# Four probability-value steps of a head pair in one block, and the output projection one round earlier

## The chip, the cores and the metric

One core of a Trainium2 chip runs the kernel. The time is device microseconds (us) of one execution; lower is better. The engines are TensorE (PE, its weight loads are shown as PEld), VectorE (DVE), ScalarE (ACT), GpSimd (POOL) and SyncE (SP), which issues most DMAs. Each runs its own list of instructions in the order written; semaphores order them against each other.

## The reference

A transformer block with adaptive layer norm on x of 4 batches x 512 tokens x 128 features, float32. Cut to what matters here:

```python
h = layernorm(x) * (1 + ca) + sa
qkv = h @ qkv_w.T                              # 16 heads of 64
scores = q @ k.T * 64 ** -0.5 + bias           # bias: 32 relative-position buckets per head
a = softmax(scores) @ v
x = x + ga * (a @ o_w.T)
h = layernorm(x) * (1 + cb) + sb
x = x + gb * experts(h)                        # 160 experts of 64, 8 per token, and a shared one
```

## The kernel before

The kernel has two phases. Attention comes first, for some 480 us; then routing, and a loop over pairs of experts. The change is in attention only.

**Tiling.** Attention works on pairs of heads: 8 pairs in each of 4 batches, 32 in a row. A pair has 8 units: 2 heads x 4 query tiles of 128 rows. For one unit:

- PE (`scores`, L407, matmuls L415 and L417) writes 128 x 512 scores to one of two PSUM banks; it waits until the bias of the unit two before is done.
- DVE (`add_bias`, L1018, instruction L1032) adds the position bias, writes `prob` in SBUF and keeps the row's extreme.
- ACT (`exponential`, L727, instruction L729) takes the exponential in place and, with a second small instruction, reads the row's sum.
- DVE (`invert_sums`, L1043, instruction L1049) inverts the sums of two units at once.
- POOL (`normalise`, L900, instruction L904) scales the unit.
- PE (`transpose_probs`, L420, instruction L426) transposes it in 4 parts into one of two PSUM banks.
- ACT (even units) or DVE (odd units) copies that bank to `PT` (`copy_probs`, L732 and L1037, both recorded at L208).

When all 8 units of a pair are in `PT`, PE runs four probability-value steps (`attend`, L430, matmuls L439), one for each tile of 128 keys. Each has two heads, whose matmuls write different halves of one bank; all four add into the same bank. DVE copies the result to `oT` (`copy_o`, L1051), and PE multiplies it with the pair's part of the output weights (`project_out`, L447, matmul L452), which adds the 8 pairs of a batch in one bank.

**Order.** Nothing is scheduled by a planner. Each engine has a function `pair(b, n)` that writes its order by hand, in four rounds of two units each; each round starts with the scores, biases and exponentials of its two units. Work of the pair before fills in: the transposes and copies of its units 4 and 5 are in round one, of 6 and 7 in round two; units 0 and 1 of the pair itself are transposed in round three, 2 and 3 in round four. Further in the rounds:

- `project_v` (PE, round two, L400), copied by ACT (`copy_v`, L738) ahead of ACT's copy of unit 6.
- `project_qk` for the pair after next (PE, round four, L389); then ACT's `qk_high` (L720, instruction L725) and DVE's `qk_low` (L1013, instruction L1015), and SP's DMAs that stack q and k. ACT runs `qk_high` after exponential 7; DVE runs `qk_low` as the last of the pair, and the next pair's bias of unit 0 behind it.
- Value steps: steps 0 and 1 of pair n-1 in round three of pair n; steps 2 and 3 in round one of pair n+1. The first step waits for the copies of units 6 and 7 and for `copy_o` of the pair before.
- `copy_o` in round one on DVE, `project_out` in round two on PE.
- At a batch's end the output is gated (`gate_y`, DVE), transposed back (`transpose_y`, PE) and added to x (`update_x`, DVE); in the next pair DVE takes the new x's statistics (`new_statistics`).

Pairs 8 and 9 of a batch in the code (`n` = 8 and 9) are pairs 0 and 1 of the next batch. The last batch has a short form (`final`), and the tail after it is written out.

Of the kernel before, what the change touches and what calls it, by code (L numbers as in the profile page):

```python
# [25 lines left out]
B, S, D = 4, 512, 128  # L26
# [6 lines left out]
QT = S // P  # L33
NT = T // P
HPAIRS = H // 2
# [20 lines left out]
def adaln_block(nc, x, emb, qkv_t, o_t, router_t, expert_bias, gate_t_in, down_t, gate_shared_t,  # L56
# [12 lines left out]
    with ctx:  # L69
# [284 lines left out]
        def _(pe):  # L354
# [75 lines left out]
            def attend(b, n, kb):  # L430

                if kb == 0:
                    for unit in (UNITS - 2, UNITS - 1):
                        pe.wait_ge(*copied(b, UNITS * n + unit))
                    pe.wait_ge(s_vc, b * HPAIRS + (2 * (n // 2) + 2))
                    if n >= 1:
                        pe.wait_ge(s_o, b * HPAIRS + n)
                for head in range(2):
                    last = nc.tensor.matmul(  # L439
                        ps[head * HD:(head + 1) * HD, BANK_O, :],  # L440
                        v_sb[:, (n // 2) % 2, kb, (n % 2) * P + head * HD:(n % 2) * P + (head + 1) * HD],
                        PT[:, n % 2, (head * QT + kb) * S:(head * QT + kb + 1) * S],
                        start=kb == 0, stop=kb == QT - 1, skip_group_check=True)
                if kb == QT - 1:
                    last.then_inc(s_pv, 1)

            def project_out(b, n):  # L447
                hp = n % HPAIRS
                pe.wait_ge(s_o, b * HPAIRS + (n + 1))
                if hp == 0:  # L450
                    pe.wait_ge(s_x2, b + (n // HPAIRS + X2_AHEAD))
                nc.tensor.matmul(ps[:, BANK_Y, :], woT[:, hp, :], oT[:, n % 2, :], start=hp == 0,  # L452
                                 stop=hp == HPAIRS - 1, skip_group_check=True).then_inc(s_ymm, 1)

            def transpose_y(b):

                pe.wait_ge(s_yg, b + 1)
                for t in range(QT):
                    last = nc.tensor.transpose(ps[:, BANK_Y, t * P:(t + 1) * P], yT[:, t * P:(t + 1) * P], ident[:, :])
                last.then_inc(s_ytr, 1)  # L460
# [58 lines left out]
            def pair(b, n, final=False):  # L519

                scores(b, n, 0)
                scores(b, n, 1)
                if n >= 2:
                    attend(b, n - 2, 2)
                    attend(b, n - 2, 3)
                if n == 0:
                    project_qk(b, 1)
                if n >= 1:
                    transpose_probs(b, n - 1, 4)
                    transpose_probs(b, n - 1, 5)  # L530

                scores(b, n, 2)
                scores(b, n, 3)
                if n == 0:
                    pe.wait_ge(w_split, 3)
                    project_v(b, 0)
                if not (final and n >= HPAIRS - 1):
                    project_v(b, n + 1)
                if n >= 2:
                    project_out(b, n - 2)  # L540
                if n >= 1:
                    transpose_probs(b, n - 1, 6)
                    transpose_probs(b, n - 1, 7)

                scores(b, n, 4)
                scores(b, n, 5)
                if n >= 1:
                    attend(b, n - 1, 0)
                    attend(b, n - 1, 1)
                transpose_probs(b, n, 0)  # L550
                transpose_probs(b, n, 1)

                scores(b, n, 6)
                scores(b, n, 7)
                if n == HPAIRS + 1:
                    transpose_y(b)
                if not (final and n >= HPAIRS - 2):
                    project_qk(b, n + 2)
                if final and n == HPAIRS - 1:
                    transpose_normed(0)  # L560
                transpose_probs(b, n, 2)
                transpose_probs(b, n, 3)
# [14 lines left out]
                    pair(b, n)  # L577
            for n in range(2, HPAIRS):
                pair(B - 1, n, True)
            attend(B - 1, HPAIRS - 2, 2)  # L580
            attend(B - 1, HPAIRS - 2, 3)
            transpose_probs(B - 1, HPAIRS - 1, 4)
            transpose_probs(B - 1, HPAIRS - 1, 5)
            project_out(B - 1, HPAIRS - 2)
# [339 lines left out]
        def _(dve):  # L924
# [30 lines left out]
            def qkv_low(n):  # L955

                k = QKV_STEPS[n]
                dve.wait_ge(w_high, n + 1)
                nc.vector.scalar_tensor_tensor(
                    out=wT[:, LOW, k * 512:(k + 1) * 512], in0=qkv_in[:, k * 512:(k + 1) * 512],  # L960
                    scalar=HD ** -0.5 if k < 2 else 1.0, in1=wT[:, HIGH, k * 512:(k + 1) * 512].bitcast(F32),
                    op0=ALU.mult, op1=ALU.subtract).then_inc(w_split, 1)
# [13 lines left out]
            def first_low(n):  # L976
                b = FIRST_ORDER[n]
                modulated_low(n, hcur if b == 0 else hT[:, b, :, :], h_full[b])
# [58 lines left out]
            def copy_probs(b, n, u):  # L1037
                dve.wait_ge(s_t, b * G + (UNITS * n + u + 1))
                if u == 1 and n >= 2:
                    dve.wait_ge(s_pv, b * HPAIRS + (n - 1))  # L1040
                copy_unit(nc.vector.tensor_copy, n, u).then_inc(s_cd, 1)

            def invert_sums(b, n, u):  # L1043

                g = UNITS * n + u
                dve.wait_ge(s_exp, b * G + (g + 2))
                if n >= 1:
                    dve.wait_ge(s_prob, b * G + (g - UNITS + 2))
                nc.vector.reciprocal(rinv[:, u:u + 2], rsum[:, u:u + 2]).then_inc(s_rinv, 1)  # L1049

            def copy_o(b, n):  # L1051
                dve.wait_ge(s_pv, b * HPAIRS + (n + 1))
                if n >= 2:
                    dve.wait_ge(s_ymm, b * HPAIRS + (n - 1))
                nc.vector.tensor_copy(oT[:, n % 2, :], ps[:, BANK_O, :]).then_inc(s_o, 1)

            def gate_y(b):

                dve.wait_ge(s_ymm, b * HPAIRS + HPAIRS)
                nc.vector.tensor_scalar(yT[:, :], ps[:, BANK_Y, :], modT[:, 2, bass.ds(b, 1)], None,  # L1060
                                        ALU.mult).then_inc(s_yg, 1)
# [10 lines left out]
            def update_x(b):  # L1072
                dve.wait_ge(s_ytr, b + 1)
                x_b = x_all[:, bass.ds(b, 1), :].rearrange("p o n -> p (o n)")
                nc.vector.tensor_tensor(x_b, x_b, ps[:, BANK_Y, :], ALU.add).then_inc(s_x2, 1)
# [52 lines left out]
            def pair(b, n, final=False):  # L1128

                add_bias(b, n, 0)  # L1130
                add_bias(b, n, 1)
                if n == 0:
                    first_low(1)
                    qk_low(b, 1)
                if n == 2 and b >= 1:
                    update_x(b - 1)
                    new_statistics(b - 1)
                if n >= 2:
                    copy_o(b, n - 2)
                if n >= 1:  # L1140
                    copy_probs(b, n - 1, 5)
                invert_sums(b, n, 0)

                add_bias(b, n, 2)
                add_bias(b, n, 3)
                if n == 0:
                    modulate(2)
                    modulate(3)
                if n >= 1:
                    copy_probs(b, n - 1, 7)  # L1150
                invert_sums(b, n, 2)
                if n == 3 and b >= 1:
                    moments(b - 1)

                add_bias(b, n, 4)
                add_bias(b, n, 5)
                if n == HPAIRS + 1:
                    gate_y(b)
                if n == 0:
                    qkv_low(3)  # L1160
                    qkv_low(4)
                    qkv_low(5)
                copy_probs(b, n, 1)
                invert_sums(b, n, 4)
                if n == 3 and b >= 1:
                    variance_eps(b - 1)

                add_bias(b, n, 6)
                add_bias(b, n, 7)
                if n == 0:  # L1170
                    first_low(2)
                    first_low(3)
                copy_probs(b, n, 3)
                invert_sums(b, n, 6)
                if not (final and n >= HPAIRS - 2):
                    qk_low(b, n + 2)
                else:
                    norm2(n - (HPAIRS - 2))
# [13 lines left out]
                    pair(b, n)  # L1192
            for n in range(2, HPAIRS):
                pair(B - 1, n, True)
            copy_o(B - 1, HPAIRS - 2)
            copy_probs(B - 1, HPAIRS - 1, 5)
            norm2(2)
            copy_probs(B - 1, HPAIRS - 1, 7)
# [115 lines left out]
```

## Time and profile before

| | |
|---|---|
| time, three runs | 978.61, 982.89 and 983.05 us; median 982.89 |
| profiled execution | span 977.4 us from the first to the last instruction; its time outside the span isn't recorded, and the shortest run is 1.2 us longer than the span |
| mean granted clock of PE | 0.997 of 2.4 GHz |
| busy over the span | PE 940.8 us (96%), PEld 684.4 (70%), DVE 770.3 (79%), ACT 681.3 (70%), POOL 402.8 (41%) |
| POOL in attention | nearly all of its work is L904, 256 instructions of 1568 ns |

The busy time of an engine is the time in which at least one of its instructions runs. Matmuls overlap and their ends are modelled, so PE's share says how continuously it is fed, not how near it is to its peak; the distance from the start of one instruction to the start of the next is the better measure of what an instruction takes from PE. The lists of waits name the engine whose semaphore came last.

### The profile page before, as it was taken

The page shows a single profiled execution, that of the slowest core. Times are in us where ns is not written, and L with a number is a line of the kernel's source. Part 1 is how long each engine was busy: PE and PEld are TensorE (multiplying, and loading weights), DVE is VectorE, ACT ScalarE, POOL GpSimd, SP SyncE. Part 2 cuts the span into 40 slices and gives each one's busy share as a digit, 9 for nine tenths or more (in the row PEclk, how much of TensorE's full clock was granted, in tenths as well). Part 3 has the DMA queues.
Part 4 walks back from the last instruction along what each step waited for, and adds up shares of the span by engine and source line. Part 5 has one row for each costly group of instructions (what it writes and reads, how often), then busy time and mean ns, then how long its engine had stood idle before and what let it go on. Part 6 is the DMA issues. An engine that isn't in the chain of part 4 may idle for free.

```text
span 977.4 us, 15761 instructions
## 1 busy us (share of the span) xinstructions
PE 940.8 (96%) x4592; PEld 684.4 (70%) x4592; DVE 770.3 (79%) x1450; ACT 681.3 (70%) x1171; POOL 402.8 (41%) x265
## 2 busy tenths in 40 slices
PE   4899999999999999999997999999999999999997
PEld 2656666666666666666543888888888888888886
DVE  5866766766676676676764999999999999999996
ACT  4656666666666666666655777877777777777775
POOL 0688888898888888898900000000000000000000
PEclk9999999999999999999999999999999999999999
DMA  7957644544553563454105999999999999999992
GB/s 217 235 161 202 166 115 103 130 100 117 130 122 78 125 152 92 104 130 101 47 18 139 224 221 220 220 219 220 218 218 220 217 219 217 221 216 220 219 218 61
DMA packets 71633, 160.57 MB, mean 164 GB/s; under 512 B 10416, under 2 KB 36336, under 8 KB 61856
## 3 DMA queue, kind: packets, MB, share of 16 engines
q1 hardware_dynamic: 70816, 158.66, 72.8%
q10 hardware_dynamic: 768, 1.31, 0.4%
q8 instruction: 24, 0.39, 0.2%
q14 instruction: 25, 0.20, 0.1%
HBM read 105.60 MB, written 2.42 MB: 111 GB/s over the span
## 4 chain that ended last, share of the span: by engine, by line
PE 88%; DVE 5%; ACT 3%; issue 2%; DMA 1%; POOL 1%; ACTq 0%; SPq 0%; DVEq 0%
PE ps L635 44%; PE ps L439 11%; PE ps L426 11%; PE ps L415 5%; PE ps L417 5%; PE ps L389 5%; PE ps L452 2%; PE ps L400 2%; ACT prob L729 1%; DVE prob L1032 1%; POOL prob L904 1%; DMA strips<-comb_rows 0%; DVE PT L208 0%; PE ps L374 0%; PE ps L485 0%
## 5 line engine op out<-in xcount | busy, mean ns | idle before, releaser
L904 POOL TENSOR_SCALAR prob<-prob,rinv 128x512 f32<-128x512 f32 x256 | 398.1, 1568 | 87.8 <-DVE rinv L1049 85.7
L729 ACT ACTIVATE prob<-prob,nmax 128x512 f32<-128x512 f32 x256 | 183.0, 716 | 138.7 <-DVE nmax L1032 138.6
L635 PE MATMUL ps<-hT,wT 128*128 128x512 f32 x960 | 243.9, 390 | 1.3 <-ACT oT L820 1.3
L1235 DVE TENSOR_TENSOR PT<-v_sb,strips 128x1024 f32<-128x1024 f32 x160 | 196.1, 1225 | 44.0 <-ACT v_sb L871 33.6
L871 ACT ACTIVATE v_sb<-ps 128x1024 f32<-128x1024 f32 x160 | 164.6, 1029 | 90.2 <-PE ps L635 89.9
L635 PEld LDWEIGHTS ps<-hT,wT 128*128 128x128 f32 x960 | 180.4, 188 | 40.5 <-issue 3.0
L635 PE MATMUL ps<-stack,wT 128*128 128x512 f32 x640 | 197.8, 391 | 4.3 <-DVE wT L1222 4.3
L208 DVE COPY PT<-ps 128x512 f32<-128x512 f32 x128 | 88.4, 691 | 135.4 <-PE ps L426 133.0
L1222 DVE TENSOR_TENSOR wT<-PT,stack 128x1024 fp32r<-128x1024 f32 x160 | 195.0, 1219 | 0.0
L863 ACT CAST stack<-PT 128x1024 fp32r<-128x1024 f32 x160 | 166.6, 1041 | 2.9 <-DVE PT L1235 2.9
L426 PEld LDWEIGHTS ps<-ident,prob 128*128 128x128 f32 x1024 | 114.4, 141 | 74.5 <-POOL prob L904 51.0
L1032 DVE CUSTOM_DVE_ANT_0 prob<-ps,strips 128x512 f32<-128x512 f32 x256 | 164.7, 680 | 1.0 <-PE ps L417 0.4
L635 PEld LDWEIGHTS ps<-stack,wT 128*128 128x128 f32 x640 | 120.5, 189 | 30.1 <-DVE wT L1222 5.2
L426 PE MATMUL ps<-ident,prob 128*128 128x128 f32 x1024 | 136.8, 276 | 1.9 <-ACT PT L208 1.6
L439 PE MATMUL ps<-PT,v_sb 128*64 128x512 f32 x512 | 123.8, 605 | 4.1 <-ACT PT L208 4.1
L415 PE MATMUL ps<-stack 128*128 128x512 f32 x256 | 112.4, 439 | 1.6 <-DVE nmax L1032 1.6
L635 PE MATMUL ps<-wT 128*128 128x512 f32 x320 | 99.0, 391 | 0.0
L208 ACT COPY PT<-ps 128x512 f32<-128x512 f32 x128 | 74.0, 578 | 17.3 <-PE ps L426 17.3
L439 PEld LDWEIGHTS ps<-PT,v_sb 128*64 128x64 f32 x512 | 31.1, 136 | 64.0 <-issue 48.1
L635 PEld LDWEIGHTS ps<-wT 128*128 128x128 f32 x320 | 60.4, 189 | 12.6
L389 PE MATMUL ps<-hcur,wT 128*128 128x512 f32 x192 | 52.0, 408 | 2.9 <-DVE hcur L973 2.9
L415 PEld LDWEIGHTS ps<-stack 128*128 128x128 f32 x256 | 48.6, 190 | 8.6 <-DVE nmax L1032 3.2
(113 smaller groups left out, 726.8 us busy)
## 6 DMA issues: line engine op xcount, KB each, us to landing
strips<-comb_rows SPq DMA_DIRECT2D x152, 512.0 KB, 12.8
stack<-qk SPq DMA_DIRECT2D x128, 256.0 KB, 3.8
k_low<-qk SPq DMA_DIRECT2D x64, 128.0 KB, 3.8
hT<-qk SPq DMA_DIRECT2D x64, 128.0 KB, 3.7
strips<-bias_rows SPq DMA_DIRECT2D x8, 896.0 KB, 5.6
strips<-in_L_ffn_w_gate SPq DMA_DIRECT2D x80, 64.0 KB, 11.2
strips<-in_L_ffn_w_down SPq DMA_DIRECT2D x80, 64.0 KB, 12.9
strips<-comb_rows SPq DMA_DIRECT2D x16, 256.0 KB, 5.7
```

The lines of the kernel that those rows point to most:

```text
L208: return copy(dst[:, :, qt * P:(qt + 1) * P], ps[:, BANK_T + u % 2, :].rearrange("p (k s) -> p k s", s=P))
L415: nc.tensor.matmul(ps[:, BANK_S + g % 2, :], stack[:, par, head, 0, qt * P:(qt + 1) * P], stack[:, par, head, 1, :], start=True, stop=False)
L426: last = nc.tensor.transpose(ps[:, BANK_T + u % 2, kb * P:(kb + 1) * P], prob[:, u, kb * P:(kb + 1) * P], ident[:, :])
L439: last = nc.tensor.matmul(ps[head * HD:(head + 1) * HD, BANK_O, :], v_sb[:, (n // 2) % 2, kb, (n % 2) * P + head * HD:(n % 2) * P + (head ...
L635: last = nc.tensor.matmul(ps[:, bank + c, :], weights(a), rows(m, c), start=start and k == 0, stop=stop and k == 2, skip_group_check=True)
L729: nc.scalar.activation(prob[:, u, :], prob[:, u, :], ACT.Exp, bias=nmax[:, u:u + 1], scale=-1.0, accum_out=rsum[:, u:u + 1]).then_inc(s_ex ...
L863: nc.scalar.copy(h_high[:, k % 4, :], weighted[:, k % 4, :]).then_inc(s_hh, 1)
L871: nc.scalar.activation(silu[:, k % 2, :], ps[:, BANK_G + 2 * half:BANK_G + 2 * half + 2, :].rearrange("p c s -> p (c s)"), ACT.Silu).then_ ...
L904: nc.gpsimd.tensor_scalar(prob[:, u, :], prob[:, u, :], rinv[:, u:u + 1], None, ALU.mult).then_inc(s_prob, 1)
L1032: nc.vector.tensor_tensor_reduce(out=prob[:, u, :], in0=ps[:, BANK_S + u % 2, :], in1=backwards, scale=-1.0, scalar=3.0e38, op0=ALU.add, o ...
L1222: nc.vector.tensor_tensor(h_low[:, k % 4, :], weighted[:, k % 4, :], h_high[:, k % 4, :].bitcast(F32), ALU.subtract).then_inc(s_hl, 1)
L1235: nc.vector.tensor_tensor(weighted[:, k % 4, :], silu[:, k % 2, :], cb[:, r, half * HALF:(half + 1) * HALF], ALU.mult).then_inc(s_mul, 1)
```

## The change

On PE, `attend` for all four key tiles of pair n-1 stands in round three of pair n, ahead of the transposes of units 0 and 1; steps 2 and 3 are gone from round one, and `project_out` of pair n-2 stands there instead of in round two. On DVE, `copy_o` moves from round one of the pair after next to round three, behind the reciprocal of unit 4 and ahead of the copy of unit 1; that reciprocal stands ahead of the copy now. At a batch's end `gate_y` moves from round three to round two, `transpose_y` from round four to round three, `update_x` from the next pair's round one to round four. In the tail two value steps and one `copy_o` fall away, since they are done in the last pair. No instruction is added or taken away in all; waits, buffers and DMAs are as before.

```diff
--- before.py
+++ after.py
@@ -521,8 +521,7 @@
                 scores(b, n, 0)
                 scores(b, n, 1)
                 if n >= 2:
-                    attend(b, n - 2, 2)
-                    attend(b, n - 2, 3)
+                    project_out(b, n - 2)
                 if n == 0:
                     project_qk(b, 1)
                 if n >= 1:
@@ -536,8 +535,6 @@
                     project_v(b, 0)
                 if not (final and n >= HPAIRS - 1):
                     project_v(b, n + 1)
-                if n >= 2:
-                    project_out(b, n - 2)
                 if n >= 1:
                     transpose_probs(b, n - 1, 6)
                     transpose_probs(b, n - 1, 7)
@@ -545,15 +542,15 @@
                 scores(b, n, 4)
                 scores(b, n, 5)
                 if n >= 1:
-                    attend(b, n - 1, 0)
-                    attend(b, n - 1, 1)
+                    for kb in range(QT):
+                        attend(b, n - 1, kb)
+                if n == HPAIRS + 1:
+                    transpose_y(b)
                 transpose_probs(b, n, 0)
                 transpose_probs(b, n, 1)
 
                 scores(b, n, 6)
                 scores(b, n, 7)
-                if n == HPAIRS + 1:
-                    transpose_y(b)
                 if not (final and n >= HPAIRS - 2):
                     project_qk(b, n + 2)
                 if final and n == HPAIRS - 1:
@@ -577,8 +574,6 @@
                     pair(b, n)
             for n in range(2, HPAIRS):
                 pair(B - 1, n, True)
-            attend(B - 1, HPAIRS - 2, 2)
-            attend(B - 1, HPAIRS - 2, 3)
             transpose_probs(B - 1, HPAIRS - 1, 4)
             transpose_probs(B - 1, HPAIRS - 1, 5)
             project_out(B - 1, HPAIRS - 2)
@@ -1133,10 +1128,7 @@
                     first_low(1)
                     qk_low(b, 1)
                 if n == 2 and b >= 1:
-                    update_x(b - 1)
                     new_statistics(b - 1)
-                if n >= 2:
-                    copy_o(b, n - 2)
                 if n >= 1:
                     copy_probs(b, n - 1, 5)
                 invert_sums(b, n, 0)
@@ -1148,20 +1140,22 @@
                     modulate(3)
                 if n >= 1:
                     copy_probs(b, n - 1, 7)
+                if n == HPAIRS + 1:
+                    gate_y(b)
                 invert_sums(b, n, 2)
                 if n == 3 and b >= 1:
                     moments(b - 1)
 
                 add_bias(b, n, 4)
                 add_bias(b, n, 5)
-                if n == HPAIRS + 1:
-                    gate_y(b)
                 if n == 0:
                     qkv_low(3)
                     qkv_low(4)
                     qkv_low(5)
+                invert_sums(b, n, 4)
+                if n >= 1:
+                    copy_o(b, n - 1)
                 copy_probs(b, n, 1)
-                invert_sums(b, n, 4)
                 if n == 3 and b >= 1:
                     variance_eps(b - 1)
 
@@ -1170,6 +1164,8 @@
                 if n == 0:
                     first_low(2)
                     first_low(3)
+                if n == HPAIRS + 1:
+                    update_x(b)
                 copy_probs(b, n, 3)
                 invert_sums(b, n, 6)
                 if not (final and n >= HPAIRS - 2):
@@ -1192,7 +1188,6 @@
                     pair(b, n)
             for n in range(2, HPAIRS):
                 pair(B - 1, n, True)
-            copy_o(B - 1, HPAIRS - 2)
             copy_probs(B - 1, HPAIRS - 1, 5)
             norm2(2)
             copy_probs(B - 1, HPAIRS - 1, 7)
```

## Rows read from the trace of the kernel before

**Rows 1.** Windows view, two stretches; first line names the columns.
```profile
core 0: us, PE busy (x) PEld busy (x) DVE busy (x) ACT busy (x) POOL busy (x), PEclk, DMA share, GB/s
174.00:288.00 114.00, 113.15 (x624) 74.73 (x624) 78.56 (x216) 75.33 (x176) 99.25 (x65) 1.00 0.49 114
500.00:540.00 40.00, 31.73 (x121) 16.75 (x122) 23.39 (x82) 24.15 (x43) 1.40 (x1) 0.98 0.41 107
```

**Rows 2.** Waits of PE, 60 to 500 us: total us, times, longest.
```profile
PE ps L439 <- ACT PT L208: 3.2, 5, 0.9
```

**Rows 3.** Timeline of PE, one pair: start, us, engine, line, operation.
```profile
207.74 0.40 PE L415 MATMUL ps<-stack 128*128 128x512 f32 x1
207.97 0.40 PE L417 MATMUL ps<-k_low,stack 128*128 128x512 f32 x1
208.30 1.94 PE L439 MATMUL ps<-PT,v_sb 128*64 128x512 f32 x8
210.17 1.09 PE L426 MATMUL ps<-ident,prob 128*128 128x128 f32 x8
...
214.21 0.47 PE L415 MATMUL ps<-stack 128*128 128x512 f32 x1
...
215.31 1.94 PE L439 MATMUL ps<-PT,v_sb 128*64 128x512 f32 x8
217.18 1.09 PE L426 MATMUL ps<-ident,prob 128*128 128x128 f32 x8
...
222.50 1.94 PE L439 MATMUL ps<-PT,v_sb 128*64 128x512 f32 x8
```

**Rows 4.** Timeline of ACT, the same pair.
```profile
214.12 0.99 ACT L725 CAST qk<-ps 128x1024 fp32r<-128x1024 f32 x1
...
218.34 0.19 ACT L729 ACTIVATION_READ_ACCUMULATOR prob<-prob,nmax 128x1 f32 x1
...
221.59 0.58 ACT L208 COPY PT<-ps 128x512 f32<-128x512 f32 x1
```

**Rows 5.** Timeline of DVE, the same pair.
```profile
211.30 0.69 DVE L208 COPY PT<-ps 128x512 f32<-128x512 f32 x1 [1.86 <-PE ps L426]
...
211.98 0.67 DVE L1032 CUSTOM_DVE_ANT_0 prob<-ps,strips 128x512 f32<-128x512 f32 x1
...
215.17 1.20 DVE L1015 TENSOR_TENSOR qk<-ps,qk 128x1024 fp32r<-128x1024 f32 x1
216.29 0.68 DVE L1032 CUSTOM_DVE_ANT_0 prob<-ps,strips 128x512 f32<-128x512 f32 x1
...
217.50 0.69 DVE L1055 COPY oT<-ps 128x512 f32<-128x512 f32 x1
218.31 0.69 DVE L208 COPY PT<-ps 128x512 f32<-128x512 f32 x1
218.91 0.16 DVE L1049 RECIPROCAL rinv<-rsum 128x2 f32<-128x2 f32 x1
218.99 0.67 DVE L1032 CUSTOM_DVE_ANT_0 prob<-ps,strips 128x512 f32<-128x512 f32 x1
```

**Rows 6.** Timeline of DVE, then PE, pair after a batch end.
```profile
174.61 0.87 DVE L1067 BATCH_NORM_STATS2 stats<-x_all 128x6 f32<-128x128 f32 x4
...
176.66 0.67 DVE L1032 CUSTOM_DVE_ANT_0 prob<-ps,strips 128x512 f32<-128x512 f32 x1
...
179.90 1.94 PE L439 MATMUL ps<-PT,v_sb 128*64 128x512 f32 x8 [0.85 <-ACT PT L208]
```

**Rows 7.** Timeline of PE, then DVE, in the tail.
```profile
493.98 3.65 PE L439 MATMUL ps<-PT,v_sb 128*64 128x512 f32 x16
497.57 0.66 PE L471 MATMUL ps<-ident,xn 128*128 128x128 f32 x4
...
497.68 0.69 DVE L1055 COPY oT<-ps 128x512 f32<-128x512 f32 x1
```

**Rows 8.** DMA issues: size of one, median us to landing.
```profile
stack<-qk SPq DMA_DIRECT2D x128, 256.0 KB, 3.8
```

## The prediction

> **What bounds the kernel now.** I read the page's slices first: the attention phase fills the first half, TensorE (PE) is at 9 tenths almost everywhere there. The change touches this phase alone; the expert loop after it keeps its code. Next I read the windows view: between 174 and 288 us PE is busy 113.15 of 114 us, VectorE (DVE) 78.56, ScalarE (ACT) 75.33, GpSimd 99.25, at a granted clock of 1.00, the 2.4 GHz level [rows 1]. So PE paces the pairs. The list of waits agrees: between 60 and 500 us the largest entry for PE is 3.2 us in 5 waits, probability-value steps (L439) that wait for ACT's copies of transposed probabilities [rows 2].
>
> But that entry names what is late next. So I followed one pair on PE and then on DVE and ACT, from one third-round block of value steps (208.30) to the next (222.50): a pair takes 14.20 us [rows 3]. Beside PE's own sequence runs a chain of hand-overs that closes on itself once in a pair:
> - value steps at 208.30, transposes of units 0 and 1 at 210.17, DVE's copy of unit 1 at 211.30 [rows 3, 5]: 3.00 us
> - to the bias of unit 6 at 211.98, with a reciprocal between [rows 5]: 0.68
> - through two exponentials to ACT's qk_high at 214.12 [rows 4]: 2.14
> - to DVE's qk_low at 215.17: 1.05; to the next pair's bias of unit 0 at 216.29: 1.12; to its bias of unit 2 at 218.99: 2.70 [rows 5]
> - through exponentials 2 and 3 and copy_v to the end of ACT's copy of unit 6 at 221.59 + 0.58 = 222.17 [rows 4]: 3.18
>
> The sum is 13.87. The next value steps start at 222.50, so this chain has 0.33 us of slack against 14.20. That is the number on which the forecast rests: four engines that stand in order, with a loop only 2% shorter than PE's work.
>
> The kernel itself shows what happens when the slack is used up. In the pair after each batch's end DVE's first round carries 4 statistics of x (0.87 us) besides; bias 2 comes at 176.66, and the value steps start at 179.90, after 0.85 us in which PE idled for ACT's copy [rows 6]. From bias 2 to value steps is 3.24 us there, which is my 3.18 plus a hand-over of about 0.05.
>
> **The change, part by part.**
>
> *One block of four value steps.* The same 16 matmuls, without a second entry. A block of all four stands in the tail already: from 493.98 to the next instruction at 497.57 is 3.59 us [rows 7], against 2 x 1.87 (208.30 to 210.17, 215.31 to 217.18) [rows 3]: 0.15 less. Entering costs too: scores follow each other at 0.23 us (207.74, 207.97), the first value step comes 0.33 after the last score [rows 3]: 0.10 less for one entry instead of two. On PE alone a pair would be 14.20 - 0.25 = 13.95 us.
>
> *What it does to the chain.* The third-round block gets longer by 3.59 - 1.87 = 1.72 us, and all of it lies on the loop, since the transposes of units 0 and 1 are queued behind it on PE, and DVE's copy of unit 1 and the biases of units 6 and 7 behind those. The first round gets shorter by as much, but that helps PE only to arrive early: from the pair's start (214.21) to the value steps (222.50) it now takes 8.29 us [rows 3], without the block of 1.87 and its entry of 0.10 some 6.3; ACT's copy of unit 6 ends at 222.17 - 214.21 = 7.96 in the present order. PE then waits.
>
> *copy_o moves from DVE's first round to its third.* In round one it stands between bias 1 and the copy of unit 5 (217.50 to 218.31) [rows 5]. Without it the reciprocal waits for the second exponential instead, whose sum is read by 218.34 + 0.19 = 218.53 [rows 4]. With a hand-over of 0.05 (the tail's copy_o starts at 497.68, 0.05 after the last value step ends at 493.98 + 3.65) [rows 7] the reciprocal comes at 218.58 and bias 2, 0.08 later, at 218.66 instead of 218.99: 0.33 less on the loop. The ends are 0.41 (no hand-over) and nothing (if the copy of unit 5 becomes late). In round three copy_o starts 3.70 us after the block's start (497.68 - 493.98) and occupies DVE for 0.6 (a copy at 211.30 and the reciprocal behind it together take 0.68); it is through at 4.3, while the copy of unit 1 can't start before 3.59 + 1.13 = 4.72 (1.13 from the transposes at 210.17 to the copy at 211.30 [rows 3, 5]). So it is hidden under the transposes; if it were not, it would cost up to 0.6 in every pair.
>
> *The reciprocal of unit 4 ahead of the copy of unit 1* takes its 0.07 (218.91 to 218.99, the same operation) off the loop [rows 5] and gives GpSimd its work earlier. GpSimd is at 87% [rows 1] and is no step of the loop.
>
> *project_out from round two to round one:* the same two matmuls, its input copied in the round before last; nothing. *gate_y, transpose_y, update_x* (three pairs, batch ends): the same instructions one round earlier or later, on DVE in places where it idles. I take nothing; uncovered they would be under 1 us each, 3 us in all. *Queues:* no DMA is added or moved on SP. Its stacks of q and k are issued behind qk_high and qk_low, land 3.8 us later [rows 8], and are first read one whole pair later, so a longer pair gives them more time.
>
> *The sum for a pair:* 13.87 + 1.72 - 0.33 - 0.07 + 0.05 (the hand-over to the value steps) = 15.24 us against 14.20: **1.04 us more**, between 0.96 (0.41 in place of 0.33) and 1.37 (nothing saved by copy_o). PE's own 13.95 lies inside it, so 1.3 us of each pair become waits of PE.
>
> The Trainium skill, "Perfetto Trace Analysis", section "Identifying the Most-Contended Engine", says that matmul busy time is a poor measure of TensorE's headroom and that the busy share of the weight loads is a good one. Here the loads are busy 74.73 of 114 us [rows 1], 66%, so by that rule PE would have a third of each pair to spare. By the row of starts, which run through the pair without a hole, it has none; the result by the rule is rival 2.
>
> *Over the run:* of 32 pairs, 30 periods (from the second pair to the last but one) hold the new block. 27 at 1.04 make 28.1. In the three that follow a batch's end DVE was late already (0.85 us of idle [rows 6]); I take 0.3 each, 0.9. For the last pair and the tail, two value steps fewer there against two more in the pair, I take nothing, between -2 and +1.7. Sum: 29 us. The profiled execution's span of 977.4 becomes 1006.4. The three runs before were 978.61, 982.89 and 983.05; the median lies 5.5 above the span, so on the median the forecast is 982.9 + 29 = **1012 us**.
>
> **The rivals.**
>
> 1. *Faster: only PE counts.* If the loop had room, 31 saved entries at 0.25 give -7.8 us: 975 us. For it speaks PE's 99% [rows 1]. It decides where the copy of unit 6 ends before PE, arriving at 6.3 us, needs it; the loop would have to be 1.3 us shorter than its rows add up to. Against it: DVE and ACT take their instructions in order, and the batch-end pairs show the same wait [rows 6]. Chance 0.05.
> 2. *No change: PE swallows the wait.* By the loads' 66%, 4.8 us of each pair would be free, and 1.3 us of waiting would fall into them: 983 us. Against it: in the batch-end pairs the wait of 0.85 stands in the open as idle time. Chance 0.03.
> 3. *Slower still: copy_o isn't covered.* If DVE came to the copy of unit 1 later by copy_o's 0.6, a pair costs 1.64 more, 27 x 1.64 + 0.9 + 3 for uncovered batch ends = 48 us: 1031 us. Against it: 0.4 us of cover by the rows above. Chance 0.05.
>
> A falling clock isn't counted: between 500 and 540 us PE is busy only 31.73 of 40 us, and the granted clock is still 0.98 [rows 1].
>
> **How the numbers follow.** The loop has 0.87. Its low end is 27 x 0.96 - 2 = 24 us on the lowest run rather than the median, 1002.6, and I allow 4 more for hand-overs that I have all at 0.05: 998. Its high end is 27 x 1.37 + 0.9 + 1.7 = 39.6: 1022. With 0.13 in the other cases this range needs no widening. Faster by over 0.5% (about what a measurement here can tell from no change) is rival 1, 0.05; within 0.5% rival 2, 0.03; slower the loop and rival 3, 0.92.
>
> **What would show it.** Right: pairs of about 15.2 us; value steps of L439 in one run of 16, some 3.6 us long; before each of them about 1 us of PE idle, ended by ACT's copy of probabilities, some 30 times in the list of waits where there were 5; small waits of PE for the bias (second round) and for ACT's copy of unit 4; on DVE a hole ahead of the first reciprocal, ended by ACT, and copy_o done before the transposes of unit 1 end. Wrong: pairs under 14.2 us, with value steps that start right behind the scores (then the loop is shorter than its rows), or copies of unit 1 that start right behind copy_o (rival 3).

## The result, and the profile after

The changed kernel takes 1014.71 us (median), the kernel before in the same comparison 982.15: slower by 3.8%, ratio 1.0383 with a 95% interval of 1.0354 to 1.0412. The forecast was 1012 in a range of 998 to 1022. Some executions of a kernel are over 1.5% slower than its fastest; the ratios here and in the table of experiments leave those out, the medians don't. By the two profiled executions the span went from 977.4 to 1012.3 us, 34.9 more. The lines of the page that answer to the table of before (first the span, then busy time and share by engine; DVE, ACT and POOL do the same work in a longer time):

```profile
span 1012.3 us, 15764 instructions
## 1 busy us (share of the span) xinstructions
PE 948.0 (94%) x4592; PEld 689.2 (68%) x4592; DVE 782.9 (77%) x1450; ACT 678.6 (67%) x1171; POOL 401.5 (40%) x265
```

The windows view of the same stretch as in [rows 1]: PE is busy 107.20 of 114 us instead of 113.15, and its granted clock is still 1.00.

```profile
174.00:288.00 114.00, 107.20 (x579) 69.71 (x578) 74.88 (x200) 68.40 (x159) 92.96 (x61) 1.00 0.45 104
```

The list of waits of PE between 60 and 500 us answers to [rows 2] (total us, times, longest). The wait that was 3.2 us in 5 times is 25.1 in 28:

```profile
PE ps L439 <- ACT PT L208: 25.1, 28, 1.1
PE ps L415 <- DVE nmax L1027: 2.5, 1, 2.5
```

And the timeline of PE over one plain pair, which answers to [rows 3]. Line numbers of the other engines have moved by 5.

```profile
220.75 3.65 PE L439 MATMUL ps<-PT,v_sb 128*64 128x512 f32 x16 [0.89 <-ACT PT L208]
224.34 1.09 PE L426 MATMUL ps<-ident,prob 128*128 128x128 f32 x8
...
227.57 1.03 PE L426 MATMUL ps<-ident,prob 128*128 128x128 f32 x8
228.36 0.48 PE L415 MATMUL ps<-stack 128*128 128x512 f32 x1
...
229.36 1.02 PE L452 MATMUL ps<-oT,woT 128*128 128x512 f32 x2
230.22 1.04 PE L426 MATMUL ps<-ident,prob 128*128 128x128 f32 x8
231.18 0.50 PE L415 MATMUL ps<-stack 128*128 128x512 f32 x1
...
233.30 1.07 PE L426 MATMUL ps<-ident,prob 128*128 128x128 f32 x8
...
234.90 0.39 PE L417 MATMUL ps<-hT,stack 128*128 128x512 f32 x1
236.17 1.08 PE L439 MATMUL ps<-PT,v_sb 128*64 128x512 f32 x4 [0.88 <-ACT PT L208]
```

Each block is 16 matmuls long and takes PE 3.59 us (220.75 to 224.34), as the block in the tail did [rows 7]. From block to block it is 15.42 us, against 14.20 before [rows 3]. PE starts its last score of round three at 234.90, and behind it stands idle for 0.88 us.

The other two engines between the same two blocks, DVE first (answers to [rows 5]):

```profile
224.45 0.69 DVE L1050 COPY oT<-ps 128x512 f32<-128x512 f32 x1 [2.03 <-PE ps L439]
225.47 0.69 DVE L208 COPY PT<-ps 128x512 f32<-128x512 f32 x1 [0.32 <-PE ps L426]
226.10 0.69 DVE L1027 CUSTOM_DVE_ANT_0 prob<-ps,strips 128x512 f32<-128x512 f32 x1
...
228.64 0.69 DVE L208 COPY PT<-ps 128x512 f32<-128x512 f32 x1 [1.23 <-PE ps L426]
229.25 0.15 DVE L1044 RECIPROCAL rinv<-rsum 128x2 f32<-128x2 f32 x1
229.32 1.20 DVE L1010 TENSOR_TENSOR qk<-ps,qk 128x1024 fp32r<-128x1024 f32 x1
230.44 0.68 DVE L1027 CUSTOM_DVE_ANT_0 prob<-ps,strips 128x512 f32<-128x512 f32 x1
...
231.66 0.68 DVE L208 COPY PT<-ps 128x512 f32<-128x512 f32 x1
232.72 0.17 DVE L1044 RECIPROCAL rinv<-rsum 128x2 f32<-128x2 f32 x1 [0.38 <-ACT prob L724]
232.91 0.69 DVE L1027 CUSTOM_DVE_ANT_0 prob<-ps,strips 128x512 f32<-128x512 f32 x1
```

then ACT (answers to [rows 4]):

```profile
228.27 0.99 ACT L720 CAST qk<-ps 128x1024 fp32r<-128x1024 f32 x1
...
235.07 0.56 ACT L737 COPY v_sb<-ps 128x512 f32<-128x512 f32 x1
235.54 0.58 ACT L208 COPY PT<-ps 128x512 f32<-128x512 f32 x1
```

Reading the loop through them: block to transposes 3.59, to the copy of unit 1 1.13, to the bias of unit 6 0.63, to qk_high 2.17, to qk_low 1.05, to the next pair's bias 0 1.12, to bias 2 2.47, to the end of ACT's copy of unit 6 3.21, to the next block 0.05. The sum is 15.42, the whole pair: no leg has slack left. copy_o starts at 224.45 and DVE is idle for 0.32 us after it, so it is covered.

Two strands meet at qk_low. The one through the biases and qk_high, which the prediction followed, is done at 229.26 (228.27 + 0.99). The other runs from the block through PE's own queue to the transposes of units 2 and 3 (227.57), DVE's copy of unit 3 (228.64) and the reciprocal (229.25). qk_low starts 0.07 us after that reciprocal, in this pair and in the other 29, and a reciprocal that didn't wait is followed as closely by a bias (218.91 to 218.99 before [rows 5]). So the two end within 0.1 us of each other, and by these rows the second is the later one.

A pair is counted from its first exponential to the next pair's. The 34.9 us are 25 plain pairs (without the first three, the three after a batch end and the last) with 1.23 each on average (30.8), the three pairs after a batch end with 0.4 each (15.61 against 15.21), the first three pairs together 2.4, and 0.4 in the last pair and the tail.

### The profile page after: what moved, and what is told of

Same layout as the page of the kernel before. It is cut to its first block, busy times and chain, and to the rows that moved or that the text cites. A ratio compares the mean times of both kernels' runs of the same rounds, so it can differ in the third digit from the quotient of the medians.

```text
span 1012.3 us, 15764 instructions
## 1 busy us (share of the span) xinstructions
PE 948.0 (94%) x4592; PEld 689.2 (68%) x4592; DVE 782.9 (77%) x1450; ACT 678.6 (67%) x1171; POOL 401.5 (40%) x265
## 4 chain that ended last, share of the span: by engine, by line
PE 69%; ACT 13%; DVE 7%; issue 7%; DMA 2%; SPq 1%; ACTq 0%; DVEq 0%
PE ps L630 41%; PE ps L439 12%; ACT prob L724 9%; PE ps L426 6%; PE ps L389 4%; DVE prob L1027 3%; PE ps L415 2%; PE ps L417 2%; ACT PT L208 2%; ACT v_sb L737 1%; DMA strips<-in_L_ffn_w_down 1%; DVE qk L1010 1%; SPq L320 1%; DVE rinv L1044 1%; PE ps L374 0%
## 5 line engine op out<-in xcount | busy, mean ns | idle before, releaser
L1230 DVE TENSOR_TENSOR PT<-v_sb,strips 128x1024 f32<-128x1024 f32 x160 | 196.0, 1225 | 43.5 <-ACT v_sb L866 34.9
L439 PE MATMUL ps<-PT,v_sb 128*64 128x512 f32 x512 | 116.9, 598 | 26.4 <-ACT PT L208 26.4
L415 PE MATMUL ps<-stack 128*128 128x512 f32 x256 | 116.1, 453 | 3.3 <-DVE nmax L1027 3.3
L439 PEld LDWEIGHTS ps<-PT,v_sb 128*64 128x64 f32 x512 | 33.8, 136 | 94.7 <-issue 54.9
L1050 DVE COPY oT<-ps 128x512 f32<-128x512 f32 x32 | 22.1, 692 | 60.5 <-PE ps L439 60.4
```

The costliest lines, as they stand in the source:

```text
L415: nc.tensor.matmul(ps[:, BANK_S + g % 2, :], stack[:, par, head, 0, qt * P:(qt + 1) * P], stack[:, par, head, 1, :], start=True, stop=False)
L439: last = nc.tensor.matmul(ps[head * HD:(head + 1) * HD, BANK_O, :], v_sb[:, (n // 2) % 2, kb, (n % 2) * P + head * HD:(n % 2) * P + (head ...
L1230: nc.vector.tensor_tensor(weighted[:, k % 4, :], silu[:, k % 2, :], cb[:, r, half * HALF:(half + 1) * HALF], ALU.mult).then_inc(s_mul, 1)
```

## The experiments

Two theories stood against each other. The loop theory: the block costs nothing as such, but it stands inside a closed chain over PE, DVE and ACT, which now sets the pair. The rivals: a block of 16 matmuls is dear in itself, or the moved copy_o, or the moved project_out. In the table, a plain pair is the distance that most pairs of the profiled execution have.

| kernel | median us | before, same chip | ratio, 95% | plain pair |
|---|---|---|---|---|
| block alone, in round three | 1023.32 | 982.86 | 1.0364 to 1.0471 | 15.43 |
| the change, copy of unit 6 ahead of copy_v | 1003.72 | 982.86 | 1.0174 to 1.0302 | 14.95 |
| before, copy of unit 6 ahead of copy_v | 976.96 | 982.86 | 0.9930 to 0.9993 | 14.17 to 14.20 |
| block at the end of round four | 991.35 | 982.86 | 1.0024 to 1.0125 | 14.54 |
| the same, copy of unit 6 ahead | 982.14 | 981.15 | 0.9984 to 1.0052 | 14.14 |
| block in round one | 972.77 | 981.31 | 0.9889 to 0.9948 | 13.94 |
| the same, copy of unit 6 ahead | 972.64 | 981.31 | 0.9850 to 0.9941 | 13.92 |
| before, copy_o with two idle copies | 1009.87 | 981.31 | 1.0227 to 1.0341 | 14.91 |
| the same, copy of unit 6 ahead | 998.12 | 981.31 | 1.0130 to 1.0255 | 14.43 |

**One part alone: the block, with all else at its old place.**

```diff
                 if n >= 1:
-                    attend(b, n - 1, 0)
-                    attend(b, n - 1, 1)
+                    for kb in range(QT):
+                        attend(b, n - 1, kb)
```

(and steps 2 and 3 out of round one and the tail.) Expected:

> The block of four value steps in round three alone; copy_o, project_out, the reciprocal of unit 4 and the batch-end pieces stay where they were before the change. Loop theory: the 1.7 us that the block adds to the loop are all there, and what the change's DVE moves gave back (copy_o out of round one, some 0.23 us; the reciprocal of unit 4, 0.07) is missing: pairs of about 15.6 to 15.7 us against 15.43 in the changed kernel, 1018 to 1023 us. Rival, copy_o in round three isn't covered and costs 0.6 us a pair: taking it out of there gives pairs of about 14.8, some 996 us. Rival, the moved project_out is what costs: back near 982.

The time is in the range, but not for the reason given: plain pairs are 15.43 us as in the changed kernel, not 15.6. So the block is the whole cost of a plain pair, and the other moves neither cost nor save there. Both rivals fall: copy_o back in round one doesn't bring 0.6 us, and project_out back in round two brings nothing. PE's waits stand in other places there, with the same pair (waits of PE, 60 to 500 us):

```profile
PE ps L415 <- DVE nmax L1027: 10.4, 28, 2.8
PE ps L426 <- ACT PT L208: 9.8, 25, 0.7
PE ps L439 <- ACT PT L208: 9.4, 28, 0.8
```

So it is the length of the loop that sets the pair, and not one particular wait. What is missing here are the batch ends: the pair after one takes 16.9 us instead of 15.61, with update_x and the statistics in round one together. That is 4.0 of the 8.3 us by which the span is longer than the changed kernel's (1020.6 against 1012.3); 2.6 more lie in the last pair and the tail. DVE's first round (timeline) shows why copy_o weighs so little:

```profile
243.16 0.69 DVE L208 COPY PT<-ps 128x512 f32<-128x512 f32 x1 [3.92 <-PE ps L426]
...
247.02 1.21 DVE L1010 TENSOR_TENSOR qk<-ps,qk 128x1024 fp32r<-128x1024 f32 x1
248.14 0.68 DVE L1027 CUSTOM_DVE_ANT_0 prob<-ps,strips 128x512 f32<-128x512 f32 x1
...
249.36 0.69 DVE L1050 COPY oT<-ps 128x512 f32<-128x512 f32 x1
249.96 0.68 DVE L208 COPY PT<-ps 128x512 f32<-128x512 f32 x1
250.56 0.16 DVE L1044 RECIPROCAL rinv<-rsum 128x2 f32<-128x2 f32 x1
250.63 0.68 DVE L1027 CUSTOM_DVE_ANT_0 prob<-ps,strips 128x512 f32<-128x512 f32 x1
```

From bias 0 to bias 2 is 2.49 us with copy_o, 2.47 without it in the changed kernel. Before it was 2.70, because the copy of unit 5 waited 0.2 us for its transposes behind copy_o; they come earlier in both kernels, since PE's first round is shorter.

**One wait shortened: ACT's copy of unit 6 ahead of copy_v.** In the changed kernel, and in the kernel before as a control:

```diff
+                if n >= 1:
+                    copy_probs(b, n - 1, 6)
                 if not (final and n >= HPAIRS - 1):
                     copy_v(b, n + 1)
-                if n >= 1:
-                    copy_probs(b, n - 1, 6)
```

> The changed kernel with ACT's copy of unit 6 ahead of copy_v in round two, nothing else. Loop theory: copy_v (0.47 us from its start to the next start) leaves the loop, the value steps start that much earlier: pairs of about 14.95 us instead of 15.43, some 13 us less, about 1001 us. Rival, the block of 16 matmuls itself costs PE the time and the wait is only where it shows: no change, 1014.7.

> The kernel before with the same swap on ACT (copy of unit 6 ahead of copy_v), as a control. Loop theory: its chain has 0.33 us of slack already, PE's own 14.20 us a pair set the time; 0.47 more of slack changes nothing in the plain pairs and saves at most about 0.5 us in the three pairs after a batch's end: 980 to 983. Rival, ACT's copy bounds the kernel before too: 13 us less, 969.

The swap takes 0.48 us off each plain pair of the changed kernel (15.43 to 14.95), about what copy_v takes of ACT, and the idle time ahead of a block goes from 0.89 to 0.39 us (timeline of PE):

```profile
216.07 3.65 PE L439 MATMUL ps<-PT,v_sb 128*64 128x512 f32 x16 [0.39 <-ACT PT L208]
```

In the kernel before, plain pairs stay at 14.17 to 14.20. It is 0.4% faster all the same, more than expected. The pairs after a batch end take 14.73 instead of 15.21 us, and the second and third pair 0.8 less together, some 2.3 us. The first pair is 0.7 us shorter, as it is in the changed kernel without the swap too. That is 3.0 of the 3.2 us by which the span is shorter (974.2 against 977.4).

**The same block elsewhere.** At the end of round four:

```diff
                 transpose_probs(b, n, 2)
                 transpose_probs(b, n, 3)
+                if n >= 1:
+                    for kb in range(QT):
+                        attend(b, n - 1, kb)
```

> The same block of four, but at the end of round four, behind the transposes of units 2 and 3; copy_o, project_out and the batch-end pieces as before the change. There no copy on DVE and no bias is queued behind it that closes the loop. Loop theory: the wait for ACT's copy of unit 6 disappears ahead of the value steps; PE alone would give 13.95 us a pair, a smaller wait ahead of the transposes of unit 0 (the bank's copy of unit 6, 0.3 us) gives some back: 13.9 to 14.2 us a pair, 973 to 982 us in all. Rival, a block of 16 is slow wherever it stands: about 1014.

The wait ahead of the value steps is gone, and 0.89 us a pair with it, so a block of 16 is not slow as such. But 991.35 is a miss. PE now waits ahead of the transposes of unit 0, and the loop closes there. The profile names GpSimd (first the waits of PE, then the timelines of PE, ACT and POOL in one pair):

```profile
PE ps L426 <- POOL prob L899: 12.9, 31, 0.9
...
224.88 1.06 PE L426 MATMUL ps<-ident,prob 128*128 128x128 f32 x8 [0.36 <-POOL prob L899]
...
224.15 0.58 ACT L208 COPY PT<-ps 128x512 f32<-128x512 f32 x1
...
221.72 6.19 POOL L899 TENSOR_SCALAR prob<-prob,rinv 128x512 f32<-128x512 f32 x4 [2.18 <-DVE rinv L1044]
```

GpSimd's unit 0, the first of the four, was done after a quarter of its 6.19 us, at 223.3, long before. ACT's copy of unit 6, which frees the bank, ends at 224.73. The next run puts it to the test, with the swap of above in this kernel:

> The block at the end of round four, and ACT's copy of unit 6 ahead of copy_v. There the profile put PE's wait ahead of the transposes of unit 0 down to GpSimd. Loop theory: it is ACT's copy of unit 6 that frees the bank (it ended 0.14 us before those transposes started, GpSimd's unit 0 had been done for 1.6 us): the copy 0.47 us earlier takes the wait of 0.36 to 0.45 away, pairs of 14.1 instead of 14.54, some 978 us. Rival, GpSimd is what is waited for: pairs stay at 14.54, 991 us.

The pairs are 14.14 us long, and the wait that was put down to GpSimd is almost gone (waits of PE, 60 to 500 us):

```profile
PE ps L426 <- ACT PT L208: 2.5, 5, 0.7
PE ps L426 <- POOL prob L899: 0.6, 2, 0.5
```

So the copy it was, and the releaser that the profile names was only the last one it saw. The time (982.14, no different from before) stays 4 us above what I expected. The pairs after a batch end still take 15.64, 0.43 more than before the change, which is 1.3 us in all; the rest isn't placed.

In round one, where only the second half stood before:

```diff
                 if n >= 2:
-                    attend(b, n - 2, 2)
-                    attend(b, n - 2, 3)
+                    for kb in range(QT):
+                        attend(b, n - 2, kb)
```

(and steps 0 and 1 out of round three; the tail runs all four.)

> The same block of four in round one of the pair after next (where steps 2 and 3 stood before), all else as before the change. Loop theory: the value steps find their copies done long before; the transposes of units 4 and 5 behind the block get late, but DVE and ACT have room there. PE's own work is left: 14.20 less one entry, 13.9 to 13.95 us a pair, 8 us under the kernel before: about 974. Rival, one block of 16 matmuls costs more than two of 8: slower than before, as the block at the end of round four was (991).

> The block of four in round one, and ACT's copy of unit 6 ahead of copy_v. If each of the two acts by itself (control of the swap: 977 against 983, the most of it in the first pairs and at the batch ends): about 970. Loop theory: nothing waits for the copy of unit 6 once the block stands in round one, so the swap adds nothing: the same as the block in round one alone, within 3 us.

Both are as the loop theory has it, and both beat the kernel before, by 0.8 and 1.0%. The block starts right behind the scores (timeline of PE):

```profile
208.75 0.48 PE L415 MATMUL ps<-stack 128*128 128x512 f32 x1
...
209.53 0.39 PE L417 MATMUL ps<-hT,stack 128*128 128x512 f32 x1
209.84 3.65 PE L439 MATMUL ps<-PT,v_sb 128*64 128x512 f32 x16
213.43 1.09 PE L426 MATMUL ps<-ident,prob 128*128 128x128 f32 x8
...
222.70 0.48 PE L415 MATMUL ps<-stack 128*128 128x512 f32 x1
```

The pair is 13.95 us (208.75 to 222.70), PE's own work with one entry saved. The list of waits has no entry for L439 any more, and the swap on ACT adds nothing. Not every pair gains that much: the 25 plain pairs are 3.7 us shorter in all, and not 25 times 0.25, because PE waits elsewhere in some, 1.06 us in one ahead of `project_qk` for a DMA. The second and third pair (3.1 us together) and the three after a batch end (2.2) gain more.

**A dose for the slack.** Two idle copies ahead of each copy_o in the kernel before, and the same with the swap on ACT:

```diff
+                for k in range(2):
+                    nc.vector.tensor_copy(spare[:, k, :], ps[:, BANK_O, :])
                 nc.vector.tensor_copy(oT[:, n % 2, :], ps[:, BANK_O, :]).then_inc(s_o, 1)
```

> The kernel before with two idle copies of the same bank added ahead of each copy_o on DVE in round one (1.2 us of DVE a pair, results unused): a dose for the slack. Loop theory: 0.33 us of slack and 0.1 us of a hole ahead of the copy of unit 5 are used up, the rest, 0.8 us a pair, shows: pairs of 15.0 us, some 1006 us, with PE waits for ACT's copy as in the changed kernel. Rival, DVE's idle 30% takes it: 983.

> The same dose, with ACT's copy of unit 6 ahead of copy_v (0.47 us off the loop). Loop theory: pairs of 14.54 us, 0.47 less than with the dose alone: some 992 us. Rival, the dose acts through something other than ACT's copy of unit 6: the same as the dose alone.

1.2 us of DVE work, in an engine that is idle for 30% of the time, lengthen the pair by 0.71 us (14.91), with the wait of the changed kernel ahead of the value steps (timelines of DVE, biases 0 and 2, and of PE; line numbers are one higher):

```profile
195.46 0.68 DVE L1033 CUSTOM_DVE_ANT_0 prob<-ps,strips 128x512 f32<-128x512 f32 x1
...
199.14 0.67 DVE L1033 CUSTOM_DVE_ANT_0 prob<-ps,strips 128x512 f32<-128x512 f32 x1
...
202.38 1.94 PE L440 MATMUL ps<-PT,v_sb 128*64 128x512 f32 x8 [0.68 <-ACT PT L209]
```

The swap takes 0.48 of it back (14.43). Both pairs are 0.1 shorter than forecast. The hole ahead of the copy of unit 5 takes up 0.2 of the dose and not 0.1: from bias 0 to bias 2 it is 0.98 longer (195.46 to 199.14), and less the slack of 0.28 (0.33 without the hand-over of 0.05) that leaves 0.70. The time of the dose alone, 1009.87, is 4 us above the expected 1006; in its profile the last pair and the tail are 7.4 us longer than before, for a reason that isn't known. The time with the swap is 998, above the expected 992; its runs scatter from 990.5 to 1004.8, and the profiled one, from which the pairs are read, is the 990.5.

## Why the prediction was right

- *PE paces the kernel before, with 0.33 us of slack in the loop.* Shown: the swap leaves the plain pairs of before as they are, and a dose of 1.2 us on DVE lengthens them by 0.71. With the hand-over of 0.05, which the sum adds at its end, the slack is 0.28.
- *The block adds 1.72 us to the loop.* Shown by the block alone, 15.43 us a pair. That it saves PE 0.25 us is shown by the block in round one, 13.95 us, the very number of the prediction.
- *PE waits for ACT's copy of unit 6, some 30 times about 1 us.* 28 times, 25.1 us; the swap cuts it by copy_v's time. Of the 1.47 us that a pair is longer than PE's own 13.95, some 0.9 stand there; the rest lies in delays in rounds one and two that are too short for the list (transposes to scores take 0.96 from 230.22 to 231.18, against 0.79 from 227.57 to 228.36).
- *copy_o is covered in round three.* Right: 0.32 us of idle DVE behind it, where 0.4 was worked out.
- *0.33 less on the loop without copy_o in round one.* Here the working was wrong, and the size came near by luck. Bias 2 did come earlier, by 0.23 instead of 0.33, but not because copy_o was gone: with copy_o in place it comes 0.21 earlier as well, because the transposes of unit 5 are. The missing 0.1 lies behind the reciprocal: one that waited for ACT is followed by the bias after 0.19 us (232.72 to 232.91), not after the 0.08 that I took from one that hadn't waited [rows 5].
- *0.07 less by the reciprocal of unit 4 ahead of the copy of unit 1.* It saved 0.02 at most: from the copy of unit 1 to qk_low it is 3.85 us in the changed kernel, 3.87 before [rows 5], and 3.86 in the block alone (243.16 to 247.02), where the reciprocal stands behind the copy. The working left out the second strand, through DVE's copy of unit 3, which this move doesn't shorten.
- *1.04 us a pair* was mis-sized by 0.18: 0.10 at bias 2, 0.05 at qk_low, and 0.03 from bias 2 to the end of ACT's copy of unit 6 (3.21 instead of 3.18). It is 1.22 in the pair shown and 1.23 on average. Over the run 29 us became 34.9.
- *0.3 in the pairs after a batch end* measured 0.4; *nothing in the last pair and the tail* measured 0.4. That the batch-end pieces cost nothing was too modest: beside the block alone they save 1.3 us in each of three pairs.
- The rivals: PE's entry is the only thing that counts (975) is what the block in round one does (972.77), so that rival had the right price for another place. PE swallowing the wait is refuted by 25.1 us of idle time; the rule on the weight loads' share (the Trainium skill, "Perfetto Trace Analysis", "Identifying the Most-Contended Engine") would have misled here. By it PE would have a third to spare in the block in round one as well, where the loads are busy 76.16 of 114 us; but there PE's steps follow each other without a hole through a pair of 13.95 us.

## What to carry to other kernels

An engine that is busy for 99% of the time may still stand next to a loop through the other engines that is only 2% shorter; add up one period leg by leg, from the starts in the timelines, before work is moved along it, and where two strands meet add up both. A saving on the busiest engine counts only where the moved work stands outside that loop: the same block of 16 matmuls made this kernel 3.8% slower in round three, and 0.8% faster in round one. Where two waits end together, the releaser in the profile is the later one by its records; swap the other one to find out.

## What the runs showed of the hardware that was not expected

In the changed kernel a small reciprocal on DVE that had to wait for ACT is followed by a bias 0.19 us after its start, in 52 cases; one that follows DVE's own work by 0.07 to 0.08. It isn't the wait alone: ahead of another small instruction (BATCH_NORM_AGGREGATE, 3 cases) the reciprocal that waited is followed after 0.08 as well. The cause stays open. PE's transposes start 0.15 us after the copy that frees their bank ends (224.73 to 224.88, in the block at the end of round four), value steps 0.05 after the copy that they wait for (236.12 to 236.17).
